# Attention in rounds of a whole third of a head instead of three groups per third, with four banks for maxima and one for the context

## The reference

```python
h = _layernorm(x, ln1_g, ln1_b)
q = (h @ wq + bq).reshape(B, S, N_HEADS, dk)          # S = 1354, N_HEADS = 8, dk = 32
k = (h @ wk + bk).reshape(B, S, N_HEADS, dk)
v = (h @ wv + bv).reshape(B, S, N_HEADS, dk)
scores = jnp.einsum('bqhd,bkhd->bhqk', q, k) / np.sqrt(dk)
attn = jax.nn.softmax(scores, axis=-1)
ctx = jnp.einsum('bhqk,bkhd->bqhd', attn, v).reshape(B, S, D)
x = x + ctx @ wo + bo
```

## Time and profile before

| | us |
|---|---|
| median of 3 runs | 997.51 |
| the runs | 995.08, 997.51, 1002.05 |
| the profiled execution, its own time | 995.35 |
| its span, first to last instruction | 993.6 |
| q/k products and values product, first slots | 84 to 132 |
| scores, exponentials, values | 132 to 369 |
| out product, norms, routing, first experts | 369 to 575 |
| second graph layer and second experts | 575 to 994 |

### The profile page before, as it was taken

One profiled execution on the slowest core, in us unless ns is written; L12 is line 12 of the kernel. 1 busy time (PEld: TensorE's weight loads), 2 busy tenths in 40 slices (PEclk: granted clock), 3 DMA queues, 4 the chain that ended last, 5 costly groups with the idle time before them and its releaser, 6 DMA issues.

```text
span 993.6 us, 12839 instructions
## 1 busy us (share of the span) xinstructions
PE 813.3 (82%) x3873; PEld 568.9 (57%) x3874; DVE 509.9 (51%) x1052; ACT 389.2 (39%) x798; POOL 112.0 (11%) x100
## 2 busy tenths in 40 slices
PE   4977899999999896149999276964459999999993
PEld 4866555555555444039999265852326666666663
DVE  4025676666666837538888238776312222222220
ACT  1005435555555654026665144212014444444441
POOL 2000200000000000350000400000711111111111
PEclk9998979999999998669999687987579999999997
DMA  7499722223331010033551483325232222222212
GB/s 264 149 275 318 190 74 72 65 42 71 80 71 37 22 32 4 32 132 109 215 196 41 143 339 117 116 84 255 91 100 32 32 32 32 32 33 32 32 27 66
DMA packets 53654, 101.57 MB, mean 102 GB/s; under 512 B 17614, under 2 KB 46054, under 8 KB 51920
## 3 DMA queue, kind: packets, MB, share of 16 engines
q1 hardware_dynamic: 47328, 92.20, 29.0%
q0 software_dynamic: 6288, 8.89, 5.0%
HBM read 70.80 MB, written 25.35 MB: 97 GB/s over the span
## 4 chain that ended last, share of the span: by engine, by line
PE 74%; issue 10%; DVE 7%; DMA 3%; ACT 2%; POOL 2%; SPq 1%; POOLq 0%; ACTq 0%; DVEq 0%
PE ps L1209 11%; PE ps L966 10%; PE ps L1191 10%; PE ps L946 7%; PE ps L895 5%; PE ps L958 5%; PE ps L1140 4%; PE ps L1056 4%; PE ps L1058 3%; PE ps L1057 3%; PE ps L1200 3%; PE ps L1155 1%; PE ps L883 1%; PE ps L919 1%; PE ps L1117 1%
## 5 line engine op out<-in xcount | busy, mean ns | idle before, releaser
L1350 DVE TENSOR_REDUCE mx<-ps 128x1 f32<-128x452 f32 x264 | 148.8, 622 | 70.2 <-PE ps L946 68.9
L743 ACT ACTIVATE expo<-ps 128x452 f32<-128x452 f32 x264 | 124.3, 551 | 89.9 <-PE ps L958 88.9
L966 PE MATMUL ps<-expo,v_st 128*64 128x452 f32 (+1 forms) x576 | 116.8, 527 | 0.0
L1209 PE MATMUL ps<-w_l,h 128*128 x464 | 109.1, 389 | 6.7 <-ACT h L866 4.1
L866 ACT ACT_TABLE_LOAD x29 | 37.2, 1283 | 189.4 <-PE ps L1200 189.4
L946 PE MATMUL ps<-k_st,q_st 96*128 96x452 f32 x264 | 105.8, 413 | 4.6 <-DVE mx L1350 2.7
L1191 PE MATMUL ps<-w_l,x1t_t 128*128 x232 | 106.0, 600 | 1.6 <-DVE x1t_t L1644 1.6
L1209 PEld LDWEIGHTS ps<-w_l,h 128*128 128x128 f32 x464 | 86.9, 192 | 24.7 <-issue 13.8
L958 PE MATMUL ps<-q_st,k_st 98*128 98x452 f32 x264 | 96.8, 387 | 2.3 <-ACT expo L743 2.0
L1656 DVE COPY h1pre<-ps 128x1024 f32<-128x1024 f32 x29 | 35.5, 1225 | 107.4 <-PE ps L1191 107.4
L946 PEld LDWEIGHTS ps<-k_st,q_st 96*128 96x128 f32 x264 | 50.8, 193 | 49.1 <-DVE mx L1350 34.9
(11 more groups left out here) (231 smaller groups left out, 1255.2 us busy)
## 6 DMA issues: line engine op xcount, KB each, us to landing
w_l<-w_l SPq DMA_DIRECT2D x8, 2053.0 KB, 8.2
w_l<-w_l SPq DMA_DIRECT2D x2, 8208.0 KB, 23.7
adj<-adj_t SPq DMA_DIRECT2D x22, 704.0 KB, 4.1
xs_d<-zeros SPq DMA_DIRECT2D x1, 3842.5 KB, 26.2
x1t<-xs_d SPq DMA_DIRECT2D x29, 132.5 KB, 2.1
q_st<-q_hi_d SPq DMA_DIRECT2D x16, 176.0 KB, 3.1
k_st<-k_hi_d SPq DMA_DIRECT2D x16, 176.0 KB, 4.1
xs_d<-zeros SPq DMA_DIRECT2D x1, 2176.0 KB, 10.4
```

Of the source, the lines that this page charges most:

```text
L743: act.activation(expo[g % 8][:, :], ps[:, 3 + g % 3, 0:QC], ACT.Exp, scale=SCALE).then_inc(s_exp, 1)
L966: return pe.matmul(ps[at:at + 2 * DK, 6 + g // T % 2, lo:hi], v_st[h % 2][:, kt, :], expo[g % 8][:, lo:hi], start=kt < 2, stop=kt == T - 1 ...
L1209: mm = pe.matmul(ps[:, 6, 0:D], h1[:, f, :], w_l1[:, bass.ds(e, 1), at:at + D].rearrange("p a n -> p (a n)"), start=f == 0, stop=f == FT - 1)
L1350: dve.tensor_reduce(mx4[:, n // KB, n % KB:n % KB + 1], ps[:, i % 3, 0:KC], AX_X, ALU.max).then_inc(s_mx, 1)
```

## The change

- One round is a whole third: `GROUPS` has 24 entries of 11 key tiles in place of 72 of 4, 4 and 3. A round issues the scores of the next third between slots, then the values of the present one. The first round's scores are interleaved with slots as well.
- Each value waits for its own exponential; before, a group waited for its last one. There are 20 `expo` buffers in place of eight.
- Slots use the banks 0, 1, 2 and 7, the context only bank 6, the q/k products 3 to 6.
- The turn slot of a head stands six chunks behind the head's last chunk in place of two (still two for head 0, none for head 7).
- SP issues the maxima of the next head ahead of the second third's stores.
- The second weight buffer `w_l0[1]` moves in memory and is loaded only after the last values of the attention.
- The out product's tile 6 waits for the last copy of the context.

```diff
-PARTS = (4, 4, 3)
+EXPOS = 20
...
         def qk_bank(n):
-            return n if n < HALF else 3 + (n - HALF) % 5
+            return n if n < HALF else 3 + (n - HALF) % 4
...
-        GROUPS = [range(third * T + sum(PARTS[:n]), third * T + sum(PARTS[:n + 1]))
-                  for third in range(H * THIRDS) for n in range(len(PARTS))]
-
-
-        TURN = [(h + 1) * CHUNKS + h + min(2, (H - 1 - h) * CHUNKS) for h in range(H)]
+        GROUPS = [range(n * T, (n + 1) * T) for n in range(H * THIRDS)]
+
+
+        TURN = [(h + 1) * CHUNKS + h + min(6 if h else 2, (H - 1 - h) * CHUNKS) for h in range(H)]
         SLOTS = H * CHUNKS + H
...
         FILL = TURN[0] + 7
+        MAX_BANKS = (0, 1, 2, 7)
         BESIDE = 4
         AHEAD = 8
 
         def slots_by(phase):
 
-            return min(SLOTS, FILL + -(-SLOTS * (phase + 1) // len(GROUPS)) + min(phase + 1, AHEAD))
+            return min(SLOTS, FILL + AHEAD + -(-SLOTS * (phase + 1) // len(GROUPS)))
...
             sp.wait_ge(s_g0_row, T)
-            for e in range(2):
-                sp.dma_start(w_l0[e][:, :], a["w_l0"][e]).then_inc(s_w0[e], 16)
+            sp.dma_start(w_l0[0][:, :], a["w_l0"][0]).then_inc(s_w0[0], 16)
...
                 store_third(h, 0)
-                store_third(h, 1)
                 if h + 1 < H:
                     load_max(h + 1)
+                store_third(h, 1)
             store_third(H - 1, 2)
+            sp.wait_ge(s_av, PRIMED + H * UNITS)
+            sp.dma_start(w_l0[1][:, :], a["w_l0"][1]).then_inc(s_w0[1], 16)
...
                 act.wait_ge(s_s2, g + 1)
-                if g >= 8:
-                    act.wait_ge(s_av, PRIMED + g - 7)
-                act.activation(expo[g % 8][:, :], ps[:, 3 + g % 3, 0:QC], ACT.Exp, scale=SCALE).then_inc(s_exp, 1)
+                if g >= EXPOS:
+                    act.wait_ge(s_av, PRIMED + g - EXPOS + 1)
+                act.activation(expo[g % EXPOS][:, :], ps[:, 3 + g % 3, 0:QC], ACT.Exp, scale=SCALE).then_inc(s_exp, 1)
...
-                act.activation(ctx_raw[n % 2][:, :], ps[:, 6 + n % 2, 0:QC], ACT.Identity).then_inc(s_cr, 1)
+                act.activation(ctx_raw[n % 2][:, :], ps[:, 6, 0:QC], ACT.Identity).then_inc(s_cr, 1)
...
-                if j and j % len(PARTS) == 0:
-                    copy_third(j // len(PARTS) - 1)
+                if j:
+                    copy_third(j - 1)
...
-                if n >= HALF + 5:
-                    pe.wait_ge(s_qk_hi, n - 4)
+                if n >= HALF + 4:
+                    pe.wait_ge(s_qk_hi, n - 3)
...
-                if i >= 3:
-                    pe.wait_ge(s_mx, i - 2)
+                if i >= 4:
+                    pe.wait_ge(s_mx, i - 3)
...
-                if first % T == 0 and first >= 2 * T:
-                    pe.wait_ge(s_cr, PRIMED + first // T - 1)
-                pe.wait_ge(s_exp, PRIMED + group[-1] + 1)
+                if first >= T:
+                    pe.wait_ge(s_cr, PRIMED + first // T)
                 for g in group:
+                    pe.wait_ge(s_exp, PRIMED + g + 1)
...
-            for g in GROUPS[0]:
-                scores(g)
-            for j, group in enumerate(GROUPS):
-                slots = list(range(slots_by(j - 1) if j else FILL, slots_by(j)))
-                for g in GROUPS[j + 1] if j + 1 < len(GROUPS) else ():
+            def next_scores(phase):
+
+                slots = list(range(slots_by(phase - 1) if phase >= 0 else FILL, slots_by(phase)))
+                for g in GROUPS[phase + 1] if phase + 1 < len(GROUPS) else ():
                     if slots:
                         fill_slot(slots.pop(0))
                     scores(g)
                 for i in slots:
                     fill_slot(i)
+
+            next_scores(-1)
+            for j, group in enumerate(GROUPS):
+                next_scores(j)
                 group_values(group)
...
                 pe.wait_ge(s_ctx, 2 + min((t * P + P - 1) // QC, THIRDS - 1))
+                if t == 6:
+                    pe.wait_ge(s_cr, PRIMED + H * THIRDS)
```

More of the change, by code:

```diff
@@ L169, in build_program @@
         cursor[0] = arena
-        w_l0 = [place(f"w_l0_{i}", [WCOLS]) for i in range(2)]
+        w_l0 = [place("w_l0_0", [WCOLS])]
         attn_at = cursor[0]
@@ L175, in build_program @@
         k_st = [place(f"k_st{i}", [NP], F32R) for i in range(3)]
-        expo = [place(f"expo{i}", [QC]) for i in range(8)]
+        expo = [place(f"expo{i}", [QC]) for i in range(EXPOS)]
         ctx_raw = [place(f"ctx_raw{i}", [QC]) for i in range(2)]
@@ L191, in build_program @@
         cursor[0] = attn_at
+        w_l0.append(place("w_l0_1", [WCOLS]))
         xs0 = [place(f"xs0_{i}", [CT, D]) for i in range(2)]
@@ L935, in fill_slot @@
             def fill_slot(i):
-                if i >= 3:
-                    pe.wait_ge(s_mx, i - 2)
+                if i >= 4:
+                    pe.wait_ge(s_mx, i - 3)
                 if i in TURN:
                     pe.wait_ge(s_hl, TURN.index(i) + 1)
-                    pe.transpose(ps[0:2 * T, i % 3, 0:P], m_hl.bitcast(F32)[:, :], ident).then_inc(s_s1, 1)
+                    pe.transpose(ps[0:2 * T, MAX_BANKS[i % 4], 0:P], m_hl.bitcast(F32)[:, :], ident).then_inc(s_s1, 1)
                 else:
@@ L945, in fill_slot @@
                         pe.wait_ge(s_stack[h % 3], h // 3 * 96 + 96)
-                    pe.matmul(ps[:, i % 3, 0:KC], q_st[h % 3][0:3 * DK, (n // KB) * P:(n // KB + 1) * P],
+                    pe.matmul(ps[:, MAX_BANKS[i % 4], 0:KC], q_st[h % 3][0:3 * DK, (n // KB) * P:(n // KB + 1) * P],
                               k_st[h % 3][0:3 * DK, (n % KB) * KC:(n % KB + 1) * KC],
@@ L965, in values @@
                 at = 2 * DK * side
-                return pe.matmul(ps[at:at + 2 * DK, 6 + g // T % 2, lo:hi], v_st[h % 2][:, kt, :], expo[g % 8][:, lo:hi],
+                return pe.matmul(ps[at:at + 2 * DK, 6, lo:hi], v_st[h % 2][:, kt, :], expo[g % EXPOS][:, lo:hi],
                                  start=kt < 2, stop=kt == T - 1, skip_group_check=True)
@@ L1346, in empty_slot @@
                         dve.wait_ge(s_mload[(h - 1) % 3], (h - 1) // 3 * 16 + 16)
-                    dve.tensor_copy(m_rows[:, :], ps[0:2 * T, i % 3, 0:P]).then_inc(s_mx, 1)
+                    dve.tensor_copy(m_rows[:, :], ps[0:2 * T, MAX_BANKS[i % 4], 0:P]).then_inc(s_mx, 1)
                 else:
                     h, n = chunk_of(i)
-                    dve.tensor_reduce(mx4[:, n // KB, n % KB:n % KB + 1], ps[:, i % 3, 0:KC], AX_X, ALU.max).then_inc(s_mx, 1)
+                    dve.tensor_reduce(mx4[:, n // KB, n % KB:n % KB + 1], ps[:, MAX_BANKS[i % 4], 0:KC], AX_X, ALU.max).then_inc(s_mx, 1)
                     if n == CHUNKS - 1:
```

## The result

The changed kernel takes 1024.91 us (median of 4 runs, 1019.71 to 1025.98), the kernel before 997.38 beside it: ratio 1.0261, 95% interval 1.0229 to 1.0294. That is 27.5 us slower; the prediction had 1006, range 998 to 1018. The direction most of the working pointed to was right, the size was not: the time lies 7 us above the range.

The account below looks back on a forecast made before the run. TensorE was taken to bound the attention, waiting for nobody. Terms -4.3 - 2.0 + 15.0 - 0.3 + 1.0 + 1.2 = +10.6 on the profiled 995.35 gave 1006 us, range 998 to 1018.

Parts of the forecast that it names:

- The index argument: Head changes: turn slot 34h + 39 opens the round needing its maxima, exposing 2.5 us for each of six heads, +15.0.
- The thirds with slots: Attention rounds beside slots: 9.36, 9.69 and 9.98 us, mean 9.68 against 9.77, over 18 thirds -1.6.
- rival (c): Long bursts in the attention: DVE does not limit them, four banks and the pause in the values suffice; 996, chance 0.08.
- Four banks for the first slots: Before the attention: slots beside q/k products go from 2.57 to 2.16 us per group, seven gaps of 0.41, -2.9.
- The single context bank: Last third of the attention: the bank must be copied before its values, 4.33 + 0.72 = 5.05 against 6.85, -1.8.
- From out product to router product: After the attention: the second third's normalizing ends 1.2 us later relative to the last value, +1.2 (0.6 to 1.8).
- The wait before each value: Attention values: satisfied waits before each of 264 values cost between nothing and 4.4 us; 1.0 taken.
- rival (a): Head changes: the clock falls at each, 5 us each, six times, +30, total 1036; chance 0.10.
- one gap of 2.68 us: Argument against the clock falling: TensorE idled 2.68 us before 379.65, yet that stage's clock was 0.99.
- the burst before each gap: Second argument against the clock falling at head changes: the matmuls before each gap are dense.
- the late thirds: Last thirds of the attention, without slots: 8.98 us against 8.51, as scores wait for ACT; three such, +1.4.
- Head 7's turn slot: Last head change: turn slot 271 is over before its round; only -0.3 us, for the swap of SP's order.

Follow-up runs that it names:

- gap-filled kernel: Changed kernel with eleven more matmuls, read by nobody, behind the transpose of each of heads 1 to 6: 1009.95 us, ratio 1.0124 to the kernel before.
- small-rounds kernel: Changed kernel with rounds of 4, 4 and 3 key tiles put back, all else of the change kept: 990.56 us, ratio 0.9938 to the kernel before.
- seven banks: Changed kernel with turn slots five chunks behind, and late scores rotating over seven banks instead of three: 988.26 us, ratio 0.9911 to the kernel before.

## Why the prediction was wrong

**Right, by its own steps.** The index argument (the turn slot is the first item of the round that needs it) and its price: 2.5 per head change, 15.0 in all, measured 2.50 to 2.52 and 15.0. It is shown three ways: one place forward takes it away, the same place in the kernel before brings it in, and filling the gap keeps it. The thirds with slots: 9.69 and 9.98 predicted, 9.66 and 9.97 measured, with TensorE waiting for DVE late in each burst, so rival (c) is out. Four banks for the first slots: DVE does 23 maxima in a row,

```profile
109.72 12.39 DVE L1357 TENSOR_REDUCE mx<-ps 128x1 f32<-128x452 f32 x23
```

one per (12.39 - 0.62)/22 = 0.535, where it paused behind every fourth. The single context bank costs the last third 0.65. In the timeline of all engines, the counterpart of the earlier trace rows:

```profile
386.49 4.39 PE L968 MATMUL ps<-expo,v_st 128*64 128x452 f32 x24 [0.65 <-ACT ctx_raw L751]
...
390.81 2.86 PE L1018 MATMUL ps<-w_attn,nt 128*128 128x256 f32 x12
390.85 0.63 DVE L1382 TENSOR_TENSOR den_even<-den_even,den_odd 128x452 f32<-128x452 f32 x1 [5.94 <-DMA den_odd<-ctx_raw]
```

**Right by luck in part.** From out product to router product the time grew by 1.3 (24.4 to 25.7), predicted 1.2. But the rows that the prediction reads give 1.8: DVE would start 5.77 - 5.05 = 0.7 behind the last value in place of 1.1 ahead of it. It starts 0.04 behind it, 1.1 later than before. And the sum over the stage does not follow from that step alone: with the same instructions there the gap-filled kernel has 24.4, as before, and the one with turn slots five behind 26.1.

**A small miss.** The wait before each value was given 1.0. The values of a third take 4.32, what they would take without it (11 x 0.38 + 0.15 = 4.33): a satisfied wait cost nothing there.

**The step that failed is rival (a), the clock.** The sum of the attention had the head changes at 2.5 us each and every other term at full clock; a fall got a chance of 0.10, on two grounds that were both bad readings. First, one gap of 2.68 us without a fall was taken as evidence that such gaps are harmless. It was one draw: of six gaps of 2.5 the clock fell behind four here, and behind five in the kernel before with its turn slot moved. The Trainium skill ("TensorE: Matmul & The Clock Gate", "Why this matters for your kernels") warns of idle gaps between bursts, and means gaps somewhat longer than these. The filled gap bears out that idle time lets the clock fall, and the measurement goes further than the page: 2.5 us were enough in four cases of six. Second, the burst before each gap was to be dense. It was (24 matmuls of values without a pause before the gap at 157), and the clock fell all the same. The rival's price was wrong as well. It was taken from the 10 us stretch of the earlier trace rows: 5 us each. The falls here were short and cost 1.4 (thirds of 13.2 against 11.8) or 2.8 us, 7 together, so even a believed rival (a) would have been 30 us where the attention lost 7 by it.

**The same blindness in the late thirds.** Their waits were worked out (8.98), but at full clock; this is the same step with a second cause. Eleven matmuls of 0.19 us of work at one per 0.44 to 0.48 are a sparse burst, and the clock falls late in it in each of the three: 10.3, so 1.3 more in each of three thirds and 380.49 to 390.81 = 10.3 in place of 9.4 for the last two runs of values, some 5 us. Short rounds have the same rate of scores only in bursts of four, and in the same stage the small-rounds kernel keeps its clock (1.00 from 340 to 363). That the fall goes with the sparse burst is shown by the seven banks, which change nothing else and remove it.

**Head 7's turn slot.** The prediction looked only at when its maxima are needed ("over before its round") and put nothing for the round that holds it. That round takes 11.04 where 9.36 is the price of one with eleven slots: 1.7 us, of idle time at the transpose and low clock behind it. Moving the slot behind the scores removed both.

**The sum.** Profile against profile the kernel is 29.4 us slower, the forecast had 10.6. The attention lost 23.1 where 13.7 were forecast (-2.0 + 15.0 - 0.3 + 1.0). Behind the router product 6.7 were lost where nothing was forecast. Ahead of the scores 3.2 were won where 4.3 were forecast, and the first graph layer began 1.5 us later. The 12 us of low clock in the attention are what was missing most: without them the time would be an estimated 1013, inside the range.

**The rest.** The 23.1 us of the attention are 15.0 of gaps, 7.0 of clock behind them, 5 of the late clock, 1.7 of head 7's round, and about -6 as a remainder, which the long rounds, the banks, the waits that cost nothing and the place of the first low stretch share; no run divides it. The 6.7 us behind the router product lie in stages whose 2323 matmuls are the same; they keep TensorE busy for 463.86 us before and 470.44 in the changed kernel. They differ in how long the clock stays low in stretches that every kernel has: behind the first graph layer

```profile
72.00:90.00 18.00, 9.47 (x32) 7.38 (x33) 10.46 (x40) 5.82 (x12) 0.00 (x0) 0.53 0.81 215
```

is the changed kernel, and the kernel with the gap filled, with the same instructions up to there, has

```profile
72.00:90.00 18.00, 9.49 (x39) 7.57 (x40) 11.60 (x42) 6.82 (x14) 0.00 (x0) 0.72 0.83 241
```

0.53 against 0.72, and 1.0 us by the first slot, counted from the start of the graph layer. Behind the router product it is alike (606.5 against 602.4 us). In the changed kernel's medians this seems to be lasting, since filling the gap gained 15 us of which the attention has only 6.6. It is not the late weight load (600.0 with it in the small-rounds kernel), and it does not go with the length of the attention (the profiled execution with seven late banks, the slowest of its four, has 606.3 behind an attention of 229.3). What sets the length of these stretches stays open; some 7 of the 27.5 us are thus located, not explained.

## What to carry to other kernels

When rounds or due times change, work out at which index each latency chain starts and at which it is needed, and let at least one block of work as long as the chain lie between: here one slot's place was worth 26.6 us, more than everything the change could win. Price an exposed wait on TensorE at its length plus the half-speed stretch behind it, and price a burst that another engine feeds or empties the same way. When one user of the accumulator banks has finished, give its banks to the other.

## What the hardware showed that I had not expected

- Idle gaps of 2.50 to 2.52 us on a TensorE that was otherwise full brought the clock to half in four of six cases, and gaps of 2.47 to 2.54 in five of six in another kernel; keeping it busy with useless matmuls during the same wait made the kernel 15 us faster, 6.6 of them in the attention.
- A stretch without a long idle gap (0.28 us once per burst in the timeline of the changed kernel's late thirds) lowers it too: scores of 0.19 us of work issued one per 0.48 us, behind which 24 matmuls took 5.4 us in place of 4.32.
- Consecutive operations overlap: ACT's exponentials of 0.55 us start every 0.44, DVE's maxima of 0.62 every 0.535.
